# A router by ranks, another order of the steady batch and another end, in a two-layer sandwich block on one core

## What is computed

```python
x = x + layernorm(attn(layernorm(x)))
x = x + layernorm(ffn(layernorm(x)))
```

```python
scores = sigmoid(x @ gate_W) * route_scale          # 8 experts
topk_scores, topk_idx = top_k(scores, 2)
topk_w = topk_scores / topk_scores.sum(-1)
gate_full = sum_k topk_w[k] * onehot(topk_idx[k])   # [.., 8], two entries non-zero
out = sum_e gate_full[e] * (gelu(x @ W1[e] + b1[e]) @ W2[e] + b2[e]) + gelu(x @ Ws1 + bs1) @ Ws2 + bs2
```

## Time and profile before

| | us |
|---|---|
| median of 3 runs | 281.3 (281.28 to 281.8) |
| the profiled execution | 281.24 |
| its span, first to last instruction | 279.5 |
| TensorE busy | 252.3 (90%), 1640 matmuls |
| VectorE busy | 234.2 (84%), 615 instructions |
| ScalarE busy | 188.7 (68%), 444 instructions |
| GpSimd busy | 88.0 (31%), 144 instructions |

### The profile page before, as it was taken

The page is one execution under the profiler, slowest core; times in us unless marked ns, Lnnn a source line. Parts: engine busy times, 40 slices in busy tenths (PEclk is TensorE's granted clock), DMA queues, the critical chain, the costliest instruction groups (busy, mean ns, idle before and its releaser), DMA issues.

```text
span 279.5 us, 4820 instructions
## 1 busy us (share of the span) xinstructions
PE 252.3 (90%) x1640; PEld 175.4 (63%) x1640; DVE 234.2 (84%) x615; ACT 188.7 (68%) x444; POOL 88.0 (31%) x144
## 2 busy tenths in 40 slices
PE   5899999895988899998978899998989799999993
PEld 5444656885435686787635686787646677884483
DVE  7799899879988867999889967999599899858933
ACT  2482256638978766949798767959798546557831
POOL 5960300045471124044562114044232132431013
PEclk9999999997999999999999999999999999999998
DMA  7437801000799954401799972101799963000012
GB/s 194 100 98 242 236 19 59 1 0 5 218 230 196 233 113 83 121 1 38 245 234 208 211 137 43 49 5 32 244 217 228 230 122 73 17 0 1 0 40 75
DMA packets 23395, 32.12 MB, mean 115 GB/s; under 512 B 3958, under 2 KB 17103, under 8 KB 23371
## 3 DMA queue, kind: packets, MB, share of 16 engines
q1 hardware_dynamic: 20346, 21.59, 27.0%
q0 software_dynamic: 3024, 10.22, 20.1%
HBM read 5.07 MB, written 2.10 MB: 26 GB/s over the span
## 4 chain that ended last, share of the span: by engine, by line
PE 56%; ACT 20%; DVE 14%; POOL 4%; issue 3%; DMA 1%; POOLq 0%; DVEq 0%; ACTq 0%
PE psH L1398 11%; PE psF L1460 7%; PE psY L1500 6%; PE psG L1320 4%; PE psA L1366 4%; PE psA L1292 4%; DVE prods L284 3%; PE psA L1500 3%; POOL rstd L468 2%; ACT squares L691 2%; ACT xn L584 2%; ACT xn L698 2%; PE psG L1486 2%; DVE prods L1021 2%; PE psH L1395 2%
## 5 line engine op out<-in xcount | busy, mean ns | idle before, releaser
L284 DVE TENSOR_TENSOR prods<-qT,kT 128x1024 f32<-128x1024 f32 (+1 forms) x48 | 50.7, 1111 | 2.7 <-PE psA L1366 1.6
L466 POOL TENSOR_SCALAR var<-ss 128x4 f32<-128x4 f32 (+1 forms) x24 | 8.3, 345 | 102.0 <-ACT squares L684 46.3
L1398 PE MATMUL psH<-ident,prods 128*128 128x128 f32 x324 | 40.0, 273 | 0.0
L468 POOL TENSOR_TENSOR rstd<-var,neg_half 128x4 f32<-128x4 f32 (+2 forms) x27 | 38.1, 1412 | 2.2
L1398 PEld LDWEIGHTS psH<-ident,prods 128*128 128x128 f32 x324 | 36.4, 141 | 2.9 <-issue 2.9
L1021 DVE TENSOR_TENSOR prods<-v_shift,prob 128x896 f32<-128x896 f32 x32 | 34.6, 1082 | 0.0
L1460 PE MATMUL psF<-x3T,w 128*128 128x512 f32 x58 | 29.4, 614 | 1.4 <-ACT hid L722 1.4
L1366 PE MATMUL psA<-prods,slot_sel 128*32 128x512 f32 x168 | 23.0, 598 | 3.4 <-DVE kv L961 2.3
L722 ACT ACTIVATE hid<-psF,b1c 128x512 f32<-128x512 f32 x29 | 19.2, 690 | 6.6 <-PE psF L1460 6.5
L1164 DVE TENSOR_TENSOR hid<-hid,psG 128x512 f32<-128x512 f32 x30 | 19.3, 681 | 3.3 <-PE psG L1486 3.3
L1021 DVE TENSOR_TENSOR prods<-v_tok,prob 128x128 f32<-128x128 f32 (+2 forms) x60 | 20.8, 369 | 0.1
(11 more groups left out here) (247 smaller groups left out, 590.9 us busy)
## 6 DMA issues: line engine op xcount, KB each, us to landing
v_shift<-v_tok SPq DMA_DIRECT2D x20, 448.0 KB
convT<-tapT POOLq DMA_DIRECT2D x6, 512.0 KB, 6.0
x_res<-L_attn_x SPq DMA_DIRECT2D x4, 512.0 KB, 9.5
out<-y_out SPq DMA_DIRECT2D x7, 256.0 KB, 2.3
x_in<-L_attn_x SPq DMA_DIRECT2D x3, 512.0 KB, 4.0
v_shift<-v_tok SPq DMA_DIRECT2D x4, 384.0 KB
tapT<-tapT POOLq DMA_DIRECT2D x3, 512.0 KB, 11.5
convT<-kexp POOLq DMA_DIRECT2D x3, 512.0 KB, 9.1
```

The source lines that it names most:

```text
L284: return eng.tensor_tensor(prods[:, QUADS * (s % 2) + q, t0:t1], qT[:, t0:t1], kT[:, PRE - off + t0:PRE - off + t1], ALU.mult)
L468: return nc.gpsimd.tensor_tensor(rstd[:, cols], var[:, cols], neg_half[:, cols], ALU.pow)
L1398: ins = pe.matmul(dst, terms[:, j % TERM_BUFS, m, :], ident[:], is_transpose=True, start=False, stop=(m == live[-1]))
```

## The change

The router: 14 steps instead of 24. Steps 3 to 5 compare each score with the other seven (256 elements a step), count how many are above it, and step 6 keeps those of rank 0 and 1. The tie-break is `tie_bar`, which is minus the smallest normal number where f < e would win a tie. The last part of the split is written without copies.

The order of the steady batch moves on all five engines. On ScalarE `normalise1(b+1)` goes from before the scores to after the exponentials and `normalise3(u1)`; the taps 2 and 3 and `norm4(u0-1)` go to the next iteration's start. On TensorE `turn_x` comes after `turn_logits(u1)`, `project_k` to tile 1, `project_q` to tile 5, `output(b, 0)` to after tile 6, the fillers 18 + 14 become 8 + 8, and an `experts_out` tile stands in the place of the last filler. On VectorE the gate steps no longer stand between the products; those of u1 go to tiles 2 to 4. On GpSimd `ln1(b+1)` goes behind `ln3(u1)`.

The end: the logits of its two units are computed token by token (`token_logits`) straight from the turned rows, so that they need neither the shared copy nor `turn_logits`. The rows of the last unit are normalised by two engines, two tiles each. The fillers there go, `finish(u0 - 1)` moves up, and the hidden chunks lie in other banks.

```diff
@@ constants
-FILL_FRONT = 5
-FILL_LAST, FILL_K, FILL_OUT = 12, 18, 14
+FILL_LOW, FILL_LAST, FILL_K, FILL_OUT = 8, 8, 8, 14
-N_GATE_STEPS = 24
+N_GATE_STEPS = 14
-LAST_BANKS = (0, 1, 2, 3, 0, 1, 2, 0)
-LAST_GATE_STEPS = (12, 15, 18, 21)
+LAST_SPLIT = 2
+LAST_BANKS = (0, 1, 3, 2, 4, 0, 1, 2)
+LAST_GATE_STEPS = (6, 9, N_GATE_STEPS, N_GATE_STEPS)
@@ gpsimd
 def last_ln3():
...
+    pool.wait_ge(last_rstd, 1)
+    nc.gpsimd.tensor_tensor(nmr3[:, cols], neg_mean[:, (B - 1) % 3, cols], rstd3[:, cols],
+                            ALU.mult).then_inc(ln3_ready, 1)
...
 if attn:
-    if more:
-        ln1(b + 1)
     if b >= 2:
         ln4(u0 - 1)
-    if b:
+    if b == 0:
+        ln1(b + 1)
+    else:
         sum_taps_first(b)
         ln3(u1)
+        if more:
+            ln1(b + 1)
         sum_taps_second(b)
@@ scalar, the loop
                     if ffn:
                         gate_logits(u0)
+                        scale_taps(b, range(2, 4))
+                        if b >= 2:
+                            norm4(u0 - 1)
                         scale_taps(b, range(4, TAPS))
-                        if more:
-                            normalise1(b + 1, range(0, TPH))
-                        norm3_squares(u1)
                     scores(b)
...
                     if ffn:
-                        if more:
-                            normalise1(b + 1, range(TPH, NT))
+                        norm3_squares(u1)
                         hidden(u0, range(0, 2))
                         gates_expert_major(u0)
+                        hidden(u0, range(2, 4))
                         gate_rows(u0)
-                        hidden(u0, range(2, 4))
                         shared_hidden(u0)
                     exponentials(b)
...
+                    if ffn:
+                        normalise3(u1)
+                        if more:
+                            normalise1(b + 1, range(0, TPH))
+                        evacuate_x3(u1)
+                        if more:
+                            normalise1(b + 1, range(TPH, NT))
+                        evacuate_shared(u1)
+                        gate_logits(u1)
                     if more:
                         evacuate_x(b + 1)
                     if ffn:
-                        normalise3(u1)
-                        evacuate_x3(u1)
-                        evacuate_shared(u1)
-                        gate_logits(u1)
+                        hidden(u1, range(0, 2))
                     if more:
                         evacuate_k(b + 1)
                     if ffn:
-                        hidden(u1, range(0, 2))
+                        hidden(u1, range(2, 4))
                         norm4(u0)
-                    if more:
-                        evacuate_q(b + 1)
-                    if ffn:
-                        scale_outputs(u0)
-                        hidden(u1, range(2, 4))
                         shared_hidden(u1)
                         gates_expert_major(u1)
                         gate_rows(u1)
+                        scale_outputs(u0)
+                    if more:
+                        evacuate_q(b + 1)
                     if more:
                         key_parts(b + 1)
...
                         norm2(2 * b + 1)
+                        evacuate_v(b + 1)
                         normalise3(2 * b)
-                        evacuate_v(b + 1)
-                        scale_taps(b + 1, range(0, 1))
                         token_major_v(b + 1)
                         evacuate_x3(2 * b)
+                        token_major_fk(b + 1)
+                        scale_taps(b + 1, range(0, 1))
+                        evacuate_shared(2 * b)
                         scale_taps(b + 1, range(1, 2))
...
@@ vector
 def last_normalise(u, tiles):
+    dve.wait_ge(ln3_ready, u + 1)
...
                     elif n == 3:
-                        ins = red(m1, score, AX_X, ALU.max)
+                        ins = tt(above, score.unsqueeze(2).to_broadcast(pair), score.unsqueeze(3).to_broadcast(pair),
+                                 ALU.subtract)
                     elif n == 4:
-                        ins = tt(eq, score, spread(m1), ALU.is_equal)
+                        ins = tt(above, above, tie_bar[:].unsqueeze(1).to_broadcast(pair), ALU.is_gt)
                     elif n == 5:
-                        ins = tt(cand, eq, first_pref[:], ALU.mult)
+                        ins = red(rank, above, AX_X, ALU.add)
                     elif n == 6:
-                        ins = red(c1, cand, AX_X, ALU.max)
+                        ins = nc.vector.scalar_tensor_tensor(out=both, in0=rank, scalar=1.5, in1=score,
+                                                             op0=ALU.is_lt, op1=ALU.mult)
...
-                    products(b, 2, range(0, 1))
-                    products(b, 2, range(1, 3), gate_step_of(u0, 0))
-                    linear_state(b, gate_step_of(u0, 2))
+                    products(b, 2)
+                    linear_state(b)
...
-                        gates(u0, range(4, 24))
+                        gates(u0, range(N_GATE_STEPS))
...
-                            if ffn and 1 <= j <= TPH:
-                                gates(u1, range(2 * (3 * (j - 1) + n), 2 * (3 * (j - 1) + n + 1)))
+                            first = 2 * (3 * (j - 2) + n - 1)
+                            if ffn and 0 <= first < N_GATE_STEPS:
+                                gates(u1, range(first, first + 2))
...
                 else:
                     last_variance()
                     residual(u1)
-                    last_normalise()
-                    gates(u0, range(0, 24))
+                    dve.wait_ge(x2_ready, upto(u1, TPH, TPH))
+                    last_normalise(u1, range(TPH, TPH + LAST_SPLIT))
+                    gates(u0, range(N_GATE_STEPS))
+                    finish(u0 - 1)
@@ tensor
+            def token_logits(u):
+                pe.wait_ge(front_free, front_count(u, X3))
+                for n, j in enumerate(unit_tiles(u)):
+                    ins = pe.matmul(front(u, LOGITS)[:, bass.ts(n, EXPERTS)], x3T[:, bass.ts(j, P)],
+                                    w1[:, 4 * P:4 * P + EXPERTS], start=True, stop=True)
+                ins.then_inc(front_full, 1)
...
                     if ffn:
-                        hidden(u0, (2,))
+                        gates_expert_major(u0)
+                        hidden(u0, range(2, 4))
                         spread_gates(u0, range(0, 2))
-                        hidden(u0, (3,))
-                    if more:
-                        turn_x(b + 1)
...
+                        keep_busy(FILL_LOW, front(u1, X3))
                         spread_gates(u0, range(2, 4))
-                    if more and ffn:
-                        pe.wait_ge(hidden_free, upto(u1, N_HIDDEN, -1))
-                        keep_busy(FILL_K, front(u1, X3))
-                    if more:
-                        project_k(b + 1)
...
+                        keep_busy(FILL_K if more else FILL_LAST, front(u1, X3))
                         turn_x3(u1)
                         experts_out(u0, (0,))
                         gate_logits(u1)
                         experts_out(u0, (1,))
                         turn_logits(u1)
-                        experts_out(u0, range(2, TPH))
+                    if more:
+                        turn_x(b + 1)
+                    if ffn:
+                        experts_out(u0, (2,))
                         hidden(u1, range(0, 2))
...
                             if j == 2:
+                                experts_out(u0, (3,))
+                            if j == 3:
                                 hidden(u1, range(2, 4))
...
-                        if more and j == 1:
+                        if more and ffn and j == 1:
+                            project_k(b + 1)
+                        if more and j == (5 if ffn else 1):
                             project_q(b + 1)
                         sum_terms(b, j)
-                        if j == TPH:
+                        if j == (6 if ffn else TPH):
                             output(b, 0)
+                        if not more and j >= 6:
+                            experts_out(u1, (j - 6,))
...
-                        keep_busy(FILL_OUT, psG[:, 1, :])
...
+                            experts_out(u1, (0,))
+                        else:
+                            keep_busy(FILL_OUT, psG[:, 1, :])
                     output(b, 1)
```

More of the change, by code:

```diff
@@ L449, in more_constants @@
                     nc.gpsimd.memset(v_shift[0:off, n, 0, :], 0.0)
-                for e in range(EXPERTS):
-                    nc.gpsimd.memset(first_pref[:, :, e:e + 1], float(EXPERTS - e))
+                nc.gpsimd.affine_select(out=tie_bar[:], in_=tie_bar[:], compare_op=ALU.is_ge, fill=0.0, base=-1,
+                                        pattern=[[1, EXPERTS], [-1, EXPERTS]], channel_multiplier=0)
```

(17 more changed lines are left out.)

200 lines of the change are left out of this document (83 added, 117 removed).

## The result

The changed kernel takes 285.88 us (median of 4 runs, 284.89 to 289.10) against 281.34: a ratio of 1.0176 (of the means, as all ratios here), interval 1.0142 to 1.021. Runs more than 1.5% above the fastest of their kernel count as slow and are left out of a ratio; of all kernels only experiment 10 has such runs, two of twelve. The profiled execution took 286.24 us with a span of 284.4.

What follows compares the result with a forecast made beforehand. Each batch's first half was taken as bound by VectorE and ScalarE, the second by TensorE. Batch 1 +0.3, batch 2 -0.7, batch 3 and end -3.3 gave -3.7 us on 281.24: 277.5, range 270.5 to 282.5.

Steps and rivals of the forecast that it cites:

- Rival 4: TensorE's clock falls in the idle 2 us before turn_x3(u1) in three batches: up to 5.2 us, 282.7; chance 0.08.
- `project_q` ... ends at R+53.9 and just fits: Steady batch's second half: project_q, behind tile 4 and add_conv, ends in time for key_parts to start at R+54.65.
- R: Start of a batch's first residual, from which times are counted; before the change 59.23, 121.24, 184.22, 240.23.
- both chains: Before key_parts: ScalarE's queue from the gelus through scale_outputs and evacuate_q; TensorE's project_q behind tile 4 and add_conv.
- the terms from the turned rows to tile 3: TensorE from R+32.3: 16.1 us before, plus 0.97 for turn_x and a 0.3 wait, given as 17.2, to R+49.5.
- the 7.6 us from the table load to the next residual: Steady batch's close: stretch from key_parts' table load, taken from the earlier trace, 176.19 to 183.8.
- rival 2: Tap sums decide add_conv: 3 us lost in batch 3, 0.5 in each steady batch, 281; chance 0.1.
- 57.0 against 56.0: Batch 3: output(b,0) waits for tiles 5 and 6, so the residual starts at R+57.0, before at R+56.0.
- first half wins 3 to 4 us, second half gives it back: Batches 1 and 2: exponentials 3 and 4 us earlier, given back as VectorE's waits; batches +0.3 and -0.7.
- rival 3: First half gives nothing, longer second half makes batches 65.3 and 66.3: +6.6 - 3.3, 284.5; chance 0.14.
- the forecast's 0.5: Chance given to the main forecast of 277.5 us, whose own range is 275 to 280.
- rival 1: The second half of a batch is not lengthened: batches of 59.0 us, time 270.9; chance 0.18.

Runs made afterwards that it cites:

- experiment 10: Experiment 8 with the old 24-step router, the second unit's steps in tiles 1 to 4: 283.41 us median of 12, 282.76 without the two slow runs.
- experiment 6: experiment 1 with project_q put ahead of tile 4 instead of tile 5, norm4 and scale_outputs left in place: 284.08 us, ratio 1.0081.
- experiment 1: The changed kernel with 20 more fillers (28 for 8) before turn_x3 of the second unit in batches 1 to 3: 284.59 us, ratio 1.0103.
- Experiments 8 and 9: The former has its own line; 9 is Experiment 8 with 8, 8, 8 fillers, 20 warm-up matmuls, none at kv: 281.48 us, ratio 1.0002.
- Experiment 8: Changed kernel with more fillers (turn_x3, kv), 26 warm-up matmuls, norm4 and scale_outputs earlier, project_q before tile 4, batch 3's output(b,0) behind tile 4: 277.49 us.
- experiment 3: The kernel before with only the 14-step router, all orders of work as before: 282.70 us, ratio 1.0035.
- the same three repairs of order: Changed kernel with norm4 and scale_outputs earlier, project_q before tile 4, batch 3's output(b,0) behind tile 4: 281.48 us without added fillers, 277.49 with.
- experiment 2: The changed kernel with the memset of tie_bar on GpSimd moved behind the identity matrix: 287.57 us, ratio 1.0238.
- experiment 12: The kernel before with 24 fillers ahead of batch 1's transposes of v, where TensorE idles 2.87 us: 281.32 us, ratio 0.9992.
- experiment 11: experiment 3 with the new end (token_logits, shared rows, new banks and order), batches in the old order: 284.12 us, ratio 1.0092.

## Why the prediction was wrong

It said 277.5 us (range 270.5 to 282.5, slower 0.22); the result is 285.9. The profiled execution is 8.7 us above the forecast.

**The clock, 3.9 us.** Start 60.84 against 59.3 in undisturbed profiles: 1.5. Batch 1, 64.39 against 63.22: 1.2. Batch 2, 65.18 against 64.03: 1.2. (The undisturbed ones are batch 1 of experiment 6, whose earlier `project_q` is worth nothing by that experiment, and batch 2 of experiment 1.) Rival 4 named the mechanism, the place (the 2 us ahead of `turn_x3(u1)`), and nearly the price of one fall (up to 1.75). The step that failed is the forecast's own term for it, none: rival 4 had only a chance of 0.08. The forecast opened an idle time of 2 us in three batches, and the earlier trace rows showed what one of 2.87 did, and I took the clock as kept. It fell in two of the three. I had also set it beside the forecast as another case, where it adds to every other error. The Trainium skill, TensorE: Matmul & The Clock Gate, part on PE-mode transpose, says that transposes don't count as busy in the same way; by that rule fillers made of transposes would be useless. Experiments 8 and 9 speak against it: with such fillers the profile has no fall in the batches and the median is 4.0 us lower. The start wasn't in my list at all.

**The order of the second part, 2.6 us.** Batches 1 and 2 without a fall take 63.2 and 64.0 against 62.3 each. The step that failed: "`project_q` ... ends at R+53.9 and just fits", and `key_parts` at R+54.65. In experiment 1's batch 2 (R = 125.43) it ends at R+55.6 and the table load stands at R+56.3. TensorE's row and ScalarE's:

```profile
179.03 1.98 PE L1277 MATMUL psA<-xnT,wqkv 128*128 128x512 f32 x4
```

```profile
179.59 1.15 ACT L769 ACTIVATE y_out<-psY,rstd 128x128 f32<-128x128 f32 x4 [0.81 <-POOL rstd L477]
180.60 1.10 ACT L587 ACTIVATE qT<-psA 128x512 f32<-128x512 f32 x2
181.72 1.28 ACT L661 ACT_TABLE_LOAD   x1
```

Two terms fed it. The exponentials end at R+31.6, not 30.6, since the gates end at R+25.1: `finish` waits 0.84 us for its root, which my walk left out. And tile 3 ends at R+50.8, not 49.5. So `add_conv` is later, tile 4 and `project_q` behind it too. I had both chains, and gave the one with the smaller margin no slack. Two slips lie beside it: the terms from the turned rows to tile 3 add up to 17.4, not 17.2, and the 7.6 us from the table load to the next residual end at 183.8, where the earlier trace rows has the residual at 184.22. The latter did no harm: in experiment 1 it is 7.7.

**Batch 3 and the end, 2.0 us.** From that residual to the last row I said 92.0 us; it took 94.0 (57.4 + 36.6). `add_conv(b,0)` of batch 3 came at R+46.1, as said, and the residual at 57.4 for 57.0. So rival 2's price didn't come, though its sign did: it was a tap sum's DMA that ended VectorE's wait there.

```profile
236.55 0.69 DVE L1053 TENSOR_TENSOR prods<-psH,convT 128x512 f32<-128x512 f32 x1 [1.63 <-DMA convT<-tapT]
```

In experiment 1's batch 3 the same landing came 0.7 us later, and the batch took 58.12 us for 57.39 at the full clock: a second difference between profiles, beside the falls. In the end the gates start at R+66.2 for 65.6, but TensorE's row shows a wait that I didn't have:

```profile
263.02 1.12 PE L1457 MATMUL psY<-x3T,w 128*128 128x512 f32 x2 [1.00 <-ACT gate_shared L587]
```

Hidden 3 stands ahead of the gates' spreads in TensorE's queue and waits for a copy on ScalarE; the first unit's last product ends at R+78.6, not 77.1. Against before, batch 3 loses 1.4 and the end gains 2.7. Experiment 8 shows the loss to be one line, which my own numbers had (57.0 against 56.0) and I took as a part of the change.

**What held.** A 256-element step takes 0.42 to 0.43 us (I took 0.44 with its gap). Of the Trainium skill, VectorE: DVE Perf Modes, section on the TRN2 errata, I had used the table's row, which gives 0.33, and the trace doesn't agree with it; the same section has (N + 151) / 0.96 ns for a float32 `tensor_tensor` (stated for 512 and 2048 elements), which gives 0.42 for 256, and with that the trace agrees. A unit's 14 steps take 3.99 us (3.96). The exponentials of batch 1 end at R+30.9 (30.6). VectorE waits 5.3 us at `add_conv` (4), the saving given back just there. The head "first half wins 3 to 4 us, second half gives it back" was right; that the second half gives back more was rival 3's outcome by another road. What the router's saving was worth depends on the order: 0.4 us in the old one, all in the end (experiment 3), and about 4.5 in the repaired one, of which 1.2 in batch 3 and 2.0 in the end are seen (experiment 10). The chances had a slip: the forecast's 0.5, rival 1's 0.18 and a third of rival 2 are 0.71 before anything is taken off, not 0.72 after it.

The start, 0.1 us later than 59.23 even without a fall, makes the rest: 3.9 + 2.6 + 2.0 + 0.1 = 8.6, of 8.7 measured.

## What to carry to other kernels

When a new order wins time on one engine, look first for the idle time that it opens on TensorE, and put fillers there before judging the order: here the same three repairs of order only drew level with the kernel before without them (281.5), and beat it with them (277.5). Where a value is copied late, list every chain that ends at the copy; if two are within a microsecond, only both repairs together show. And read the single runs: clusters 1.4 to 1.7 us apart went with the mean granted clock here, as far as it shows the falls, and the median alone mixes them with the order's own worth. A stretch that is undisturbed in one batch doesn't speak for the others: the old router cost nothing in batch 1 and 1.2 us in batch 3.

## What was not expected of the hardware

The same idle time of TensorE (3.12 us, same instructions around it) was followed by the full clock in the changed kernel's profile and by a granted clock of 0.50 to 0.60 in experiment 1's. With one 0.14 us memset moved (experiment 2) the falls came in other places and the median was 1.7 us higher. In stretches of 2 us the granted clock was below 1.00 for 4 to 6 us in most falls, and for 12 in the longest (experiment 10). A short one cost 0 us where VectorE set the pace (experiment 12; in experiment 6 batch 2 has a fall at 128 to 132 us and takes 64.03 like the undisturbed one) and 1.2 to 1.8 us where TensorE did. At the start five of the profiles show the first two projection matmuls at 1.9 to 2.1 us, where the kernel before needs 1.13. TensorE's row of the changed kernel, and busy time by stretch there:

```profile
10.35 2.02 PE L1287 MATMUL psA<-xnT,wqkv 128*128 128x512 f32 x2
```

```profile
10.00:12.00 2.00, 2.00 (x4) 0.85 (x4) 1.84 (x3) 0.00 (x0) 2.00 (x7) 1.00 0.21 18
```

In four of the five the granted clock is given as 1.00 in this stretch, in experiment 11 as 0.50. So the durations told of the fall where the clock's column did not; that these four are falls of the clock is read from the equal durations, not shown by the clock.
